# A two-layer GRU with a mixture of experts: products of 256 columns issued as two calls of 128, in both halves of a slot

## The chip, the cores and the metric

The kernel runs on one core of a Trainium2 chip, in float32 throughout. The metric is the device time of one execution in microseconds (us). The engines are named as in the profile: PE is the matrix engine, PEld its weight loads, DVE the vector engine, ACT the scalar engine, POOL the general engine and SP the engine whose queue issues the DMAs.

## The reference, cut to what matters

Batch B = 2, T = 1024 time steps, D = 256 features.

```python
mixed = tanh(x @ W_in.T + b_in + cond)                 # for all steps
h1 = gru_layer(mixed, Wih0, Whh0, bih0, bhh0)          # 1024 steps, one after the other
h2 = gru_layer(h1, Wih1, Whh1, bih1, bhh1)
x = x + (gate * h2 + h2) @ W_out.T + b_out
# the mixture, for each of the 2048 tokens
shared = silu(x @ w1) * (x @ w3) @ w2                  # 512 hidden features
s = sigmoid(concat(x, 0) @ router_W)                   # 8 experts, the top 2 are chosen
routed = sum_e combine[e] * (gelu(x @ W1e[e]) @ W2e[e])
out = x + (shared + routed) / 3
```

In a GRU layer each step needs the state of the step before (`r`, `z` and `n` from `h @ Whh.T`), so 1024 steps of each layer follow each other. Everything else, the mixture above all, can be computed for many steps at once.

## The kernel before, in words

**Slots.** The program is fully unrolled: every instruction is issued once. It is written as a sequence of slots. Slot s holds step s of layer 0 and step s - 19 of layer 1 (`LAG` is 19). On PE a slot is (`pe_slots`): layer 0's step (`recur`), at a few slots a projection for layer 1, then whatever the mixture has planned for "part 0" of the slot, then layer 1's step, at a few slots a projection for layer 0, then the mixture's "part 1". The other engines have the same order. With j = s mod 16, the projections stand at j = 0 and 1 in part 0 (layer 1) and at j = 4 and 12 in part 1 (layer 0). They are 192 columns wide.

**A step.** PE multiplies the state (2 columns of weights per step done in the chunk of 16, up to 32) with the recurrent weights: `recur` issues first the reset gate's product (64 columns, L325) and then the others (128 columns, L333); where `r_first` is false (j = 4 and 12, after slot 896 also 0 and 8) one product of 192 columns does both. DVE transposes the results (L395, L404, L405), ACT takes tanh (L466, L472, L476), DVE scans (L413) and a last DVE scan, L424, makes the new state, for which the next step's product of the same layer waits.

**The mixture.** Steps are cut into groups (`GROUPS`: six of 128 steps, then 112, 80 and 64). When a group's states are there (24 slots after its last step) its mixture begins and is spread over a window of slots as long as the next group: 128 slots for the groups 0 to 4, 112 for group 5, then 80, 64 and 64. A token is a column; a group of 128 steps has TG = 256 of them. One product of the mixture is `by_columns` (L272): four matmuls, one for each strip of 32 output features, with TG columns each. In the trace each matmul is two weight loads and two passes over the columns, so a product is 8 LDWEIGHTS and 8 MATMUL records. A group has 94 products: 4 for the output layer, 2 for the router (one matmul each, not four), 48 `up` and 40 `down`.

**The plan.** `Mixture.add` gives every operation of the mixture a half-slot (two to a slot) by its dependences and by `busy`, which names the half-slots an engine may not use. A group is `sparse` when its window has 128 slots or more, that is the groups 0 to 4: then PE may take part 0 only (and not at j = 0 and 1), ACT part 0 only. A PE operation stands at least two half-slots after an operation of another engine on which it waits. For these groups the plan puts the 94 products in 94 of the 112 allowed part 0 places; part 1 holds none. In the windows of groups 6 to 8 both parts may be used; group 5 has 12 products in part 1.

**SP and the weights of the experts.** When the router's result `comb_t` is there (half-slot 84 of the window), SP writes it to DRAM, and one slot later reads it back to all partitions (`c_all`, 1 MB in the SBUF for 256 tokens). The experts' results wait for it (`mix.transfer`: 12 half-slots).

Of the kernel before, what the change touches and what calls it, by code (L numbers as in the profile page):

```python
# [12 lines left out]
KT = D // P  # L13
# [4 lines left out]
CH = 16  # L18
ROWS = CH * B
# [6 lines left out]
HS, E, HE = 512, 8, 256  # L26
# [22 lines left out]
def projection_pieces(l):  # L49

    return {4: 0, 12: 1} if l == 0 else {0: 0, 1: 1}
# [9 lines left out]
class Mixture:  # L61


    def __init__(self, first, steps, window):
        self.first, self.end, self.steps, self.window = first, first + steps, steps, window
        self.begin = self.end + LAG + 5
        self.sparse = window >= GROUPS[0]
        self.pieces = range(2 if steps > 5 * CH else 1)
        self.y_done = f"y{KT - 1}{self.pieces[-1]}"
        self.ops = {k: [] for k in ("pe", "act", "dve")}  # L70
        self.when, self.value, self.engine, self.signals = {}, {}, {}, {}
# [19 lines left out]
    def busy(self, engine, h):  # L91

        j, part = (h // 2 + self.begin) % CH, h % 2
        if engine == "pe":
            return j in projection_pieces(part ^ 1) or part == 1 and (self.sparse or self.window > 5 * CH and j % 8 != 6)
        if engine == "act":
            return ((j - LAG) if part else j) % CH == 2 or self.sparse and part == 1
        return (j, part) in ((13, 0), (1, 1), (2, 1))
# [22 lines left out]
def gru_moe_kernel(nc, a, out):  # L121
    with ExitStack() as ctx:
# [509 lines left out]
        def mixture_at(eng, engine, s, part, base):  # L632

            mix = in_window(s)
            if mix is None:
                return
            h = (s - mix.begin) * 2 + part
            for at, name, waits, issue in mix.ops[engine]:
                if at != h:
                    continue  # L640
                for w in waits:
                    wait_for(eng, mix, w)
                half = h // mix.window
                if name == "out00" and mix is mixtures[0]:
                    eng.wait_ge(s_mld, 16 * len(late_loads))
                    eng.wait_ge(s_mix, B * NTB * KT)
                if name == "out00" and mix is not mixtures[0]:
                    eng.wait_ge(m_sets[1]["dve"], before(mix).value[before(mix).y_done])
                if name == "out00":
# [21 lines left out]
        def plan(mix, x2, y, mid, score_th, scores, comb_t, c_all, by_tok, top, rest, equal, lead, mask, sel, denom, big, recip,  # L671
# [6 lines left out]
            def tokens(q):  # L678
                return slice(TH * q, TH * q + TH)

            for m in range(KT):
                for kt in range(KT):
                    mix.add("pe", f"out{m}{kt}", (), lambda pe, col, m=m, kt=kt: by_columns(
                        pe, ups[0][:, m], feature_tile(w_out[:, kt], m), hist[:, kt, bass.ds(col + ROWS, TG)], m == kt == 0, kt == KT - 1))
            for m in range(KT):
                for q in mix.pieces:
                    mix.add("dve", f"x2{m}{q}", (f"out{KT - 1}{KT - 1}",), lambda v, col, m=m, q=q: v.scalar_tensor_tensor(  # L687
                        x2[:, m, tokens(q)], ups[0][:, m, tokens(q)], b_out[:, m:m + 1],
                        x_t[:, m, bass.ds(col + TH * q, TH)], ALU.add, ALU.add), even=True)
            for kt in range(KT):  # L690
                mix.add("pe", f"route{kt}", (f"x2{KT - 1}{LAST}",), product(ups[1][0:E, 0], w_r[:, kt], x2[:, kt], kt == 0, kt == KT - 1))
            for b in range(B):
                mix.add("act", f"score{b}", (f"route{KT - 1}",), lambda act, col, b=b: act.activation(
                    score_th[:, b::B], ups[1][0:E, 0, b::B], ACT.Tanh, bias=r_bias[:, b:b + 1], scale=0.5))

            def up(u):
                kind, i = UNITS[u]
                free = () if u == 0 else ("score1",) if u == 1 else (f"act{u - 2}_1" if UNITS[u - 2][0] == "e" else f"hid{u - 2}_{LAST}",)
                for h in range(2):
                    for kt in range(KT):  # L700
                        if kind == "s":
                            w = feature_tile((w_1, w_3)[h][:, kt], i)
                        else:
                            w = feature_tile(w_1e[:, i, kt], h)
                        mix.add("pe", f"up{u}_{h}{kt}", free if h == kt == 0 else (),
                                product(ups[u % 2][:, h], w, x2[:, kt], h == kt == 0, kt == KT - 1))

            def nonlinear(u):
                kind, i = UNITS[u]
                bank, done = ups[u % 2], f"up{u}_{1}{KT - 1}"  # L710
                read = () if u < 2 or kind == "e" and mix is mixtures[-1] else (last_hid(u - 2),)
                if kind == "s":

# [21 lines left out]
            def last_hid(u):  # L735
                return f"hid{u}_{LAST}" if UNITS[u][0] == "s" else f"hid{u}_{KT - 1}{LAST}"
# [11 lines left out]
            def down(u):  # L748
                kind, i = UNITS[u]
                tiles = [w_2[:, i]] if kind == "s" else [w_2e[:, i, kt] for kt in range(KT)]  # L750
                for k, w in enumerate(tiles):
                    for m in range(KT):
                        last = k == len(tiles) - 1 and m == KT - 1
                        name = f"down{u}" if last else f"down{u}_{k}{m}"
                        mix.add("pe", name, (last_hid(u),) if k == m == 0 else (),
                                product(acc[:, m], feature_tile(w, m), hid[u % 2][:, k], u == k == m == 0, u == len(UNITS) - 1 and last))


            per_expert = [32, NB, E]
# [253 lines left out]
```

## Time and profile before

| | us |
|---|---|
| Median of three runs | 2193.89 |
| Lowest and highest | 2191.00, 2194.55 |
| Span of the profiled execution | 2185.8 |
| PE, PEld, DVE, ACT, POOL busy in it | 2068.4, 1485.0, 1841.5, 1201.4, 560.5 |

The page gives no time of the profiled execution apart from its span, from the first to the last instruction. The runs' times hold some 5 to 9 us around the span (2191.00 - 2185.8 to 2194.55 - 2185.8).

A busy PE is not a PE at its peak: matmuls are pipelined and their ends are modelled. What counts for this kernel is how long a slot takes, and what stands in the gaps of PE between one layer's step and the other's. The granted TensorE clock stands at 2.4 GHz, 0.99 to 1.00 of it, in all stretches shown below.

### The profile page before, as it was taken

What the parts mean: (1) busy time and instruction counts of PE and PEld (TensorE: products, weight loads), DVE (VectorE), ACT (ScalarE), POOL (GpSimd) and SP (SyncE); (2) the same over time, 40 slices, a digit from 0 to 9 for tenths busy, and PEclk for the clock granted to TensorE, in tenths of its full rate; (3) what the DMA queues carried; (4) which work ended last, traced back from release to release, by engine and by line L of the source; (5) the groups of instructions that cost most, each with busy time, mean ns of one, the idle gap of its engine ahead of it and who ended that gap; (6) DMA issues with size and microseconds to landing.
All of it is one profiled execution on the core that took longest, in us unless ns stands there. A gap on an engine that the chain in (4) does not pass through costs nothing.

```text
span 2185.8 us, 162058 instructions
## 1 busy us (share of the span) xinstructions
PE 2068.4 (95%) x69920; PEld 1485.0 (68%) x69920; DVE 1841.5 (84%) x11225; ACT 1201.4 (55%) x6471; POOL 560.5 (26%) x2542
## 2 busy tenths in 40 slices
PE   6989899999999999999999999999999999999987
PEld 3666666677666776767767676666767676777766
DVE  4888889888888888888888888888888888888874
ACT  2555555555555555555555555555555555555542
POOL 1222232222322223222222222222232222222220
PEclk9999999999999999999999999999999999999999
DMA  5000000000000000000000000000000000000000
GB/s 219 4 4 5 4 5 5 24 5 5 9 5 24 5 5 10 5 24 5 10 5 24 5 5 9 5 24 5 5 10 5 24 5 10 5 21 9 5 16 19
DMA packets 10879, 32.76 MB, mean 15 GB/s; under 512 B 1368, under 2 KB 6832, under 8 KB 9136
## 3 DMA queue, kind: packets, MB, share of 16 engines
q1 hardware_dynamic: 10160, 22.38, 2.8%
q8 instruction: 548, 8.98, 1.7%
q14 instruction: 171, 1.40, 0.2%
HBM read 20.22 MB, written 2.16 MB: 10 GB/s over the span
## 4 chain that ended last, share of the span: by engine, by line
PE 60%; DVE 26%; ACT 10%; issue 3%; DMA 1%; SPq 0%; POOL 0%; DVEq 0%; POOLq 0%
PE bank L333 29%; PE bank L325 17%; PE bank L272 11%; DVE n_first L404 9%; DVE cells L424 7%; ACT factors L472 6%; ACT cells L476 4%; DVE r_pre L395 4%; DVE z_pre L405 3%; PE bank L306 3%; DVE bank L413 1%; DVE n_second L380 0%; DVE x L687 0%; PE bank L657 0%; DVE hid L745 0%
## 5 line engine op out<-in xcount | busy, mean ns | idle before, releaser
L333 PE MATMUL bank<-w_h,cells 128*22 128x128 f32 (+4 forms) x32768 | 1363.4, 281 | 23.6 <-DVE cells L424 13.9
L333 PEld LDWEIGHTS bank<-w_h,cells 128*22 128x22 f32 (+4 forms) x32768 | 853.0, 111 | 130.5 <-DVE cells L424 91.3
L325 PEld LDWEIGHTS bank<-w_h,cells 128*2 128x2 f32 (+15 forms) x28112 | 512.2, 113 | 528.1 <-DVE cells L424 502.8
L517 POOL TENSOR_SCALAR cells<-cells 128x4 f32<-128x4 f32 x2048 | 463.6, 226 | 1525.8 <-DVE cells L424 1524.8
L325 PE MATMUL bank<-w_h,cells 128*2 128x64 f32 (+15 forms) x28112 | 770.1, 225 | 76.3 <-DVE cells L424 55.5
L466 ACT ACTIVATE n_second<-r_pre 128x4 f32<-128x4 f32 x2048 | 426.3, 208 | 508.8 <-DVE r_pre L395 466.3
L472 ACT ACTIVATE factors<-z_pre 128x4 f32<-128x4 f32 x2048 | 429.6, 210 | 436.5 <-DVE z_pre L405 358.8
L404 DVE STREAM_TRANSPOSE n_first<-bank 128x64 f32<-128x64 f32 x2048 | 600.0, 293 | 33.1 <-PE bank L333 23.7
L424 DVE TENSOR_TENSOR_SCAN cells<-factors,cells 128x18 f32<-128x18 f32 x2048 | 397.2, 194 | 241.5 <-ACT cells L476 177.1
L395 DVE STREAM_TRANSPOSE r_pre<-bank 128x64 f32<-128x64 f32 x2048 | 480.6, 235 | 33.3 <-PE bank L325 24.9
L405 DVE STREAM_TRANSPOSE z_pre<-bank 128x64 f32<-128x64 f32 x2048 | 427.4, 209 | 0.0
L413 DVE TENSOR_TENSOR_SCAN bank<-n_first,n_second 128x12 f32<-128x12 f32 x2048 | 396.7, 194 | 5.3 <-ACT n_second L466 1.1
L476 ACT ACTIVATE cells<-bank 128x8 f32<-128x8 f32 x2048 | 367.6, 180 | 1.4 <-DVE bank L413 0.2
L272 PE MATMUL bank<-x,w_1e 128*32 128x256 f32 (+3 forms) x2304 | 162.3, 357 | 2.3 <-issue 2.3
L272 PE MATMUL bank<-hid,w_2e 128*32 128x256 f32 (+3 forms) x2304 | 157.6, 356 | 1.8 <-DVE hid L745 1.8
L306 PE MATMUL bank<-w_x,stage 128*32 128x192 f32 x2048 | 131.9, 327 | 1.6 <-DVE z_pre L405 0.9
L272 PE MATMUL bank<-x,w 128*32 128x256 f32 (+3 forms) x1152 | 81.9, 356 | 0.2 <-DVE hid L721 0.2
L272 PEld LDWEIGHTS bank<-x,w_1e 128*32 128x32 f32 x2304 | 73.2, 110 | 2.6 <-issue 0.3
L272 PEld LDWEIGHTS bank<-hid,w_2e 128*32 128x32 f32 x2304 | 70.2, 110 | 5.4 <-DVE hid L745 2.4
L306 PEld LDWEIGHTS bank<-w_x,stage 128*32 128x32 f32 x2048 | 63.9, 109 | 14.2 <-DVE z_pre L405 1.4
L745 DVE TENSOR_TENSOR hid<-act_t,c_all 128x128 f32<-128x128 f32 (+2 forms) x240 | 66.4, 277 | 1.2 <-issue 0.7
L478 ACT ACTIVATE bank<-biases 128x256 f32<-128x256 f32 x124 | 47.5, 383 | 0.0
(91 smaller groups left out, 558.8 us busy)
## 6 DMA issues: line engine op xcount, KB each, us to landing
c_all<-weights SPq DMA_DIRECT2D x6, 1024.0 KB
x_t<-in_x_t SPq DMA_DIRECT2D x4, 512.0 KB, 7.4
w_1e<-in_w_1e SPq DMA_DIRECT2D x1, 2048.0 KB
w_2e<-in_w_2e SPq DMA_DIRECT2D x1, 2048.0 KB
w_x<-in_w_x SPq DMA_DIRECT2D x2, 768.0 KB, 8.2
w_h<-in_w_h SPq DMA_DIRECT2D x2, 768.0 KB, 9.5
w<-in_w SPq DMA_DIRECT2D x3, 512.0 KB
out_y<-y SPq DMA_DIRECT2D x6, 256.0 KB, 3.5
```

Of the source, the lines that this page charges most:

```text
L272: mm = pe.matmul(ps[strip], w[:, strip], x, start=start, stop=stop, tile_position=(0, 32 * g), skip_group_check=True)
L325: mm = pe.matmul(r_sums[l][p][32 * g:32 * g + B * (j + 1)], state_tile(l, j, kt), w_h[l][:, kt, g, 2 * U:], start=False, stop=False, tile_ ...
L333: mm = pe.matmul(sums[l][p][32 * g:32 * g + B * (j + 1), 0:width], state_tile(l, j, kt), w_h[l][:, kt, g, 0:width], start=False, stop=Fals ...
L395: v.transpose(r_pre[l][:].rearrange("p i b -> p b i"), blocks(at)).then_inc(s["turn"], 1)
L404: v.transpose(n_first[l][:, :, :, 2].rearrange("p i b -> p b i"), blocks(sums[l][p][:, 0:U])).then_inc(s["for_n"], 1)
L405: v.transpose(z_pre[l][:].rearrange("p i b -> p b i"), blocks(sums[l][p][:, U:2 * U])).then_inc(s["turn"], 1)
L413: v.tensor_tensor_scan(n_scan[l], n_first[l][:, own].rearrange("p i b e -> p (i b e)"), n_second[l][p][:, own].rearrange("p i b e -> p (i ...
L424: v.tensor_tensor_scan(step_cells(l, (j + 1) % CH, 0), factors[l][:, 2:], step_cells(l, j), 0.0, ALU.mult, ALU.add)\
L466: act.activation(n_second[l][p][:, own, :, 0], r_pre[l][:, own], ACT.Tanh, scale=0.5).then_inc(s["for_n"], 1)
L472: act.activation(cell_part(factors[l][:], 2), z_pre[l][:, own_rows(j)], ACT.Tanh, scale=0.5)
L476: act.activation(to, n.to_broadcast([P, B, UB, 2]), ACT.Tanh).then_inc(s["for_h"], 1)
L517: pool.tensor_scalar(cell_part(step_rows(l, j), 3), cell_part(step_rows(l, j), 1), 0.5, None, ALU.mult)\
```

## The change

For the sparse groups only (0 to 4), every product of 256 columns becomes two calls with 128 columns each (`mix.cuts` has two elements, `cut(c)` is the half of the columns). A group then has 188 PE operations, and each call loads its weights anew. `busy` no longer keeps PE out of part 1 for sparse groups: only the projections' places are closed (j = 0 and 1 in part 0, j = 4 and 12 in part 1). The two halves of a product have consecutive places, so that one mostly stands behind layer 0's step and the other behind layer 1's. For the other groups nothing changes (one cut, and the same rule for part 1 as before). ACT and DVE keep their operations and their rules; they wait for the second half of a product.

By the planner's rules the 188 calls get 94 places in part 0 and 94 in part 1; 81 slots of a window have both, 26 have one. Thirteen calls a window stand in part 1 of the slots j = 0 and 1, behind layer 1's projection and step. `comb_t` moves from half-slot 84 to 86, so both of SP's DMAs for it come one slot later, and the last result from half-slot 236 to 240 (of 256), and its store with it.

```diff
         self.sparse = window >= GROUPS[0]
         self.pieces = range(2 if steps > 5 * CH else 1)
+        self.cuts = self.pieces if self.sparse else range(1)
...
         if engine == "pe":
-            return j in projection_pieces(part ^ 1) or part == 1 and (self.sparse or self.window > 5 * CH and j % 8 != 6)
+            return j in projection_pieces(part ^ 1) or part == 1 and 5 * CH < self.window < GROUPS[0] and j % 8 != 6
...
+            TC, CUT = TG // len(mix.cuts), mix.cuts[-1]
+
+            def cut(c):
+                return slice(TC * c, TC * c + TC)
+
             for m in range(KT):
-                for kt in range(KT):
-                    mix.add("pe", f"out{m}{kt}", (), lambda pe, col, m=m, kt=kt: by_columns(
-                        pe, ups[0][:, m], feature_tile(w_out[:, kt], m), hist[:, kt, bass.ds(col + ROWS, TG)], m == kt == 0, kt == KT - 1))
+                for c in mix.cuts:
+                    for kt in range(KT):
+                        mix.add("pe", f"out{m}{c}{kt}", (), lambda pe, col, m=m, kt=kt, c=c: by_columns(
+                            pe, ups[0][:, m, cut(c)], feature_tile(w_out[:, kt], m), hist[:, kt, bass.ds(col + ROWS + TC * c, TC)],
+                            m == kt == c == 0, kt == KT - 1))
...
                 for h in range(2):
-                    for kt in range(KT):
...
-                        mix.add("pe", f"up{u}_{h}{kt}", free if h == kt == 0 else (),
-                                product(ups[u % 2][:, h], w, x2[:, kt], h == kt == 0, kt == KT - 1))
+                    for c in mix.cuts:
+                        for kt in range(KT):
...
+                            mix.add("pe", f"up{u}_{h}{c}{kt}", free if h == kt == c == 0 else (),
+                                    product(ups[u % 2][:, h, cut(c)], w, x2[:, kt, cut(c)], h == kt == c == 0, kt == KT - 1))
...
-                bank, done = ups[u % 2], f"up{u}_{1}{KT - 1}"
+                bank, done = ups[u % 2], f"up{u}_{1}{CUT}{KT - 1}"
...
                     for m in range(KT):
-                        last = k == len(tiles) - 1 and m == KT - 1
-                        name = f"down{u}" if last else f"down{u}_{k}{m}"
-                        mix.add("pe", name, (last_hid(u),) if k == m == 0 else (),
-                                product(acc[:, m], feature_tile(w, m), hid[u % 2][:, k], u == k == m == 0, u == len(UNITS) - 1 and last))
+                        for c in mix.cuts:
+                            last = k == len(tiles) - 1 and m == KT - 1 and c == CUT
+                            name = f"down{u}" if last else f"down{u}_{k}{m}{c}"
+                            mix.add("pe", name, (last_hid(u),) if k == m == c == 0 else (),
+                                    product(acc[:, m, cut(c)], feature_tile(w, m), hid[u % 2][:, k, cut(c)], u == k == m == c == 0,
+                                            u == len(UNITS) - 1 and last))
```

The router's products are cut in the same way.

## Rows read from the trace of the kernel before

**Rows 1.** The page: its span, PE's records, and the chain's shares by engine.

```profile
span 2185.8 us, 162058 instructions
...
PE 2068.4 (95%) x69920; PEld 1485.0 (68%) x69920; DVE 1841.5 (84%) x11225; ACT 1201.4 (55%) x6471; POOL 560.5 (26%) x2542
...
PE 60%; DVE 26%; ACT 10%; issue 3%; DMA 1%; SPq 0%; POOL 0%; DVEq 0%; POOLq 0%
```

**Rows 2.** Timeline: start, length, engine, line, operation; idle time before in brackets.

```profile
1004.21 0.61 PE L272 MATMUL bank<-x,w_1e 128*32 128x256 f32 x8
...
1004.61 0.25 PEld L325 LDWEIGHTS bank<-w_h,cells 128*6 128x6 f32 x16 [0.27 <-DVE cells L424]
...
1004.86 0.62 PE L333 MATMUL bank<-w_h,cells 128*6 128x128 f32 x16
```

**Rows 3.** Stretches: length, each engine's busy time (records); layer 1's last 16 steps, alone.

```profile
2119.52:2151.63 32.11, 21.54 (x672) 15.65 (x672) 16.97 (x89) 9.72 (x51) 4.10 (x19) 1.00 0.01 3
```

**Rows 4.** The same view: slots 32 to 151, then the five windows of 128 slots.

```profile
81.84:321.79 239.95, 215.43 (x7449) 146.78 (x7448) 203.18 (x1231) 134.92 (x736) 65.71 (x298) 1.00 0.02 5
321.79:581.67 259.88, 253.83 (x8677) 180.44 (x8676) 227.34 (x1397) 149.54 (x807) 69.86 (x316) 1.00 0.03 10
581.67:842.12 260.45, 254.62 (x8677) 180.98 (x8676) 227.48 (x1397) 148.29 (x806) 69.66 (x316) 1.00 0.03 10
842.12:1107.56 265.44, 257.13 (x8677) 184.12 (x8676) 227.84 (x1396) 148.50 (x806) 69.61 (x316) 0.99 0.03 10
1107.56:1371.42 263.86, 255.04 (x8676) 181.60 (x8676) 227.95 (x1396) 148.52 (x806) 69.62 (x316) 1.00 0.03 10
1371.42:1635.85 264.43, 256.57 (x8677) 183.13 (x8676) 228.26 (x1396) 148.75 (x806) 69.72 (x316) 0.99 0.03 10
```

**Rows 5.** The same view, of the scans L424 alone: their number in slots 32 to 151.

```profile
81.84:321.79 239.95, 46.96 (x240) 1.00 0.02 5
```

**Rows 6.** Stretches of two slots (j = 9, 10): no product, 256 columns, 160 twice, 224 twice.

```profile
1935.59:1939.54 3.95, 3.48 (x128) 2.43 (x128) 3.34 (x22) 2.20 (x12) 0.90 (x4) 1.00 0.05 14
648.75:652.68 3.93, 3.93 (x148) 2.85 (x144) 3.69 (x24) 2.12 (x12) 0.91 (x4) 1.00 0.03 6
2068.79:2072.74 3.95, 3.90 (x160) 3.29 (x160) 3.58 (x25) 2.21 (x12) 0.91 (x4) 1.00 0.02 6
1969.16:1973.21 4.05, 4.05 (x160) 3.47 (x160) 3.84 (x26) 2.40 (x14) 0.91 (x4) 1.00 0.02 4
```

**Rows 7.** Single slots j = 0: without and with 256 columns in the slot before.

```profile
597.80:599.74 1.94, 1.88 (x72) 1.43 (x72) 1.62 (x12) 1.10 (x6) 0.95 (x5) 1.00 0.00 0
629.91:631.89 1.98, 1.98 (x76) 1.44 (x72) 1.92 (x13) 1.14 (x7) 0.95 (x5) 1.00 0.03 8
```

**Rows 8.** Single slots j = 2: without products, and with 160 columns behind slot 1's projection.

```profile
2087.01:2089.00 1.99, 1.71 (x68) 1.24 (x64) 1.73 (x12) 1.06 (x6) 0.46 (x2) 1.00 0.87 277
2053.84:2055.93 2.09, 2.09 (x88) 1.83 (x84) 2.03 (x13) 1.31 (x7) 0.46 (x2) 1.00 0.00 0
```

**Rows 9.** A group's busy us and mean ns; instruction queue (packets, MB): page, first window.

```profile
L272 PEld LDWEIGHTS bank<-x,w_1e 128*32 128x32 f32 x2304 | 73.2, 110 | 2.6 <-issue 0.3
...
q8 instruction: 548, 8.98, 1.7%
...
q8 instruction: 68, 1.11, 1.8%
```

**Rows 10.** Waits of PEld in the third, fourth and fifth window: us, times, longest.

```profile
PEld bank L325 <- issue: 3.1, 3, 2.7
...
PEld bank L325 <- issue: 2.4, 1, 2.4
...
PEld bank L325 <- issue: 3.1, 3, 2.5
```

**Rows 11.** DMA share in tenths, 929.5 to 943 in 40 slices; timeline of what follows.

```profile
DMA  0000210000000009599999851100000000020000
...
940.35 0.31 PEld L325 LDWEIGHTS bank<-w_h,cells 128*8 128x8 f32 x14 [2.73 <-issue]
```

More of the change, by code:

```diff
@@ L643, in mixture_at @@
                 half = h // mix.window
-                if name == "out00" and mix is mixtures[0]:
+                if name == "out000" and mix is mixtures[0]:
                     eng.wait_ge(s_mld, 16 * len(late_loads))
                     eng.wait_ge(s_mix, B * NTB * KT)
-                if name == "out00" and mix is not mixtures[0]:
+                if name == "out000" and mix is not mixtures[0]:
                     eng.wait_ge(m_sets[1]["dve"], before(mix).value[before(mix).y_done])
-                if name == "out00":
+                if name == "out000":
                     eng.wait_ge(sets[1][mix.end // CH % 2]["pool"] if mix is not mixtures[-1] else s_hist, 2)
@@ L679, in tokens @@
                 return slice(TH * q, TH * q + TH)
+            TC, CUT = TG // len(mix.cuts), mix.cuts[-1]
+            def cut(c):
+                return slice(TC * c, TC * c + TC)
             for m in range(KT):
-                for kt in range(KT):
-                    mix.add("pe", f"out{m}{kt}", (), lambda pe, col, m=m, kt=kt: by_columns(
-                        pe, ups[0][:, m], feature_tile(w_out[:, kt], m), hist[:, kt, bass.ds(col + ROWS, TG)], m == kt == 0, kt == KT - 1))
+                for c in mix.cuts:
[3 more added lines that the diff above has]
+                            m == kt == c == 0, kt == KT - 1))
             for m in range(KT):
                 for q in mix.pieces:
-                    mix.add("dve", f"x2{m}{q}", (f"out{KT - 1}{KT - 1}",), lambda v, col, m=m, q=q: v.scalar_tensor_tensor(
+                    mix.add("dve", f"x2{m}{q}", (f"out{KT - 1}{CUT}{KT - 1}",), lambda v, col, m=m, q=q: v.scalar_tensor_tensor(
                         x2[:, m, tokens(q)], ups[0][:, m, tokens(q)], b_out[:, m:m + 1],
                         x_t[:, m, bass.ds(col + TH * q, TH)], ALU.add, ALU.add), even=True)
-            for kt in range(KT):
-                mix.add("pe", f"route{kt}", (f"x2{KT - 1}{LAST}",), product(ups[1][0:E, 0], w_r[:, kt], x2[:, kt], kt == 0, kt == KT - 1))
+            for c in mix.cuts:
+                for kt in range(KT):
+                    mix.add("pe", f"route{c}{kt}", (f"x2{KT - 1}{LAST}",),
+                            product(ups[1][0:E, 0, cut(c)], w_r[:, kt], x2[:, kt, cut(c)], kt == c == 0, kt == KT - 1))
             for b in range(B):
-                mix.add("act", f"score{b}", (f"route{KT - 1}",), lambda act, col, b=b: act.activation(
+                mix.add("act", f"score{b}", (f"route{CUT}{KT - 1}",), lambda act, col, b=b: act.activation(
                     score_th[:, b::B], ups[1][0:E, 0, b::B], ACT.Tanh, bias=r_bias[:, b:b + 1], scale=0.5))
@@ L699, in up @@
                 for h in range(2):
[L700 to L704, printed above, removed]
-                        mix.add("pe", f"up{u}_{h}{kt}", free if h == kt == 0 else (),
-                                product(ups[u % 2][:, h], w, x2[:, kt], h == kt == 0, kt == KT - 1))
+                    for c in mix.cuts:
+                        for kt in range(KT):
+                            if kind == "s":
+                                w = feature_tile((w_1, w_3)[h][:, kt], i)
+                            else:
+                                w = feature_tile(w_1e[:, i, kt], h)
+                            mix.add("pe", f"up{u}_{h}{c}{kt}", free if h == kt == c == 0 else (),
+                                    product(ups[u % 2][:, h, cut(c)], w, x2[:, kt, cut(c)], h == kt == c == 0, kt == KT - 1))
             def nonlinear(u):
                 kind, i = UNITS[u]
-                bank, done = ups[u % 2], f"up{u}_{1}{KT - 1}"
+                bank, done = ups[u % 2], f"up{u}_{1}{CUT}{KT - 1}"
                 read = () if u < 2 or kind == "e" and mix is mixtures[-1] else (last_hid(u - 2),)
@@ L752, in down @@
                     for m in range(KT):
-                        last = k == len(tiles) - 1 and m == KT - 1
-                        name = f"down{u}" if last else f"down{u}_{k}{m}"
-                        mix.add("pe", name, (last_hid(u),) if k == m == 0 else (),
-                                product(acc[:, m], feature_tile(w, m), hid[u % 2][:, k], u == k == m == 0, u == len(UNITS) - 1 and last))
+                        for c in mix.cuts:
+                            last = k == len(tiles) - 1 and m == KT - 1 and c == CUT
[3 more added lines that the diff above has]
+                                            u == len(UNITS) - 1 and last))
             per_expert = [32, NB, E]
```

## The prediction

> **What bounds the kernel now.** I read the page's chain first: PE holds 60% of it, DVE 26%, ACT 10% [rows 1]. That looks like a kernel bound by PE, where smaller or better placed products would pay. So the next view is one slot of the timeline. A product of 256 columns stands behind layer 0's step (0.61 us), and yet PE's weight loads then sit idle for 0.27 us until layer 1's scan L424 has made the state [rows 2]. PE waits for the recurrence, not the other way round. The third view is layer 1 alone, after layer 0 has ended: 16 steps in 32.11 us, 2.007 us a step [rows 3]. Now both layers together, with no product of the mixture on PE: slots 32 to 151 hold 240 scans, so 120 slots [rows 5], in 239.95 us [rows 4], 2.000 us a slot. One layer alone is no faster than two: a slot's length is the latency of one step through PE, DVE and ACT, and the other layer and the mixture live in its gaps.
>
> The change touches the five windows of 128 slots. At 2.000 us a slot each would last 255.95 us. They last 259.88, 260.45, 265.44, 263.86 and 264.43 us [rows 4]. The excess is 3.9, 4.5, 9.5, 7.9 and 8.5, together 34.3 us. That is all that could be won in them, whatever is done to the mixture, and 1.6% of the span of 2185.8 us [rows 1].
>
> **What the excess is made of.** Not the columns: two slots without a product take 3.95 us, two with 256 columns in part 0 take 3.93 us [rows 6]. It is in the waits named "issue", in which PE waits for nothing that a semaphore shows. At L325 alone they make 3.1 us in three waits in the third window; the longest one of the third, fourth and fifth window is 2.7, 2.4 and 2.5 us [rows 10]. The one of 2.7 us explains the mechanism: the broadcast of `c_all` fills the DMA engines for the ten slices that start with a 9 and end with a 1 (0.34 us each, 934.6 to 937.9), and PE stands until 940.35 [rows 11]. What PE lacks is instructions. The instruction queue q8 moved 548 packets with 8.98 MB [rows 9], that is 16 KB each; PE and PEld together have 2 x 69,920 = 139,840 records [rows 1], over 548 that is 255. I read a packet as a block of 256 PE instructions. An instruction stream of 124.1 records a slot without products ((7449 + 7448) / 120) costs no excess, one of 135.6 with them ((8677 + 8676) / 128) costs 34.3 us in 640 slots [rows 4]. I take the long waits (2.7 + 2.4 + 2.5 = 7.6 us) as collisions with `c_all`'s DMA, and the other 26.7 us as blocks that came a little late.
>
> The Trainium skill has a rule that speaks the other way: the page "Runtime: NRT & Kernel Launch", section "Instruction fetch mechanics", says that the sequencer loads 16 KiB blocks of 256 instructions ahead of time and that crossing a block is "mostly hidden". The block's size agrees with this trace (16 KB, 255 records); that it is hidden does not, by the issue waits just named. By that rule the term for late blocks below would be 0 and the time that of the second rival.
>
> **The change part by part.**
>
> *Columns and weight loads on PE.* The four strips' 128-column passes of L333, 16 records, take 0.62 us; the 256-column product, 8 records, 0.61 us [rows 2]. Sixteen records of 128 columns move as many columns as eight of 256, so a product cut in two costs PE 0.01 us more, and its eight further weight loads (110 ns each [rows 9], overlapping the passes) run beside. 470 products x 0.01 = 5 us of PE time, beside waits of 0.27 us a slot half: 0 on the path. Without that cover it would be 5 us.
>
> *Part 0 gets shorter.* A 256-column product pushes layer 1's step, and where a short slot follows this shows: j = 0 takes 1.98 us with a product in the slot before, 1.94 without [rows 7]. The plan has 6 such places a window, 30 in all: 30 x 0.045 = -1.4 us. Elsewhere the push costs nothing (3.93 against 3.95 us). After this layer 0's latency is what stands, unchanged.
>
> *Part 1 gets 128 columns.* The trace has no 128-column product behind layer 1's step, but it has wider ones: two slots with 160 columns in both parts take 3.95 us, as long as none; with 224 columns in both 4.05 us [rows 6]. So the gap closes between 160 and 224 and 128 fits: 0 for 405 of the 470 new places. The bound above is a tenth of the 224-column price per slot, 0.05 / 5 = 0.01 us, 4 us in all. The other 65 (13 a window) stand behind layer 1's projection and step at j = 0 and 1. Behind such a one with 160 columns the slot took 2.09 instead of 1.99 us [rows 8]. For 128 columns between 0 and 0.10; I take the half, 65 x 0.05 = +3.3 us (0 to 6.5).
>
> *The instruction stream.* 92 of the 94 products add 16 records, the router's two add 4: 1480 a window, 11.6 a slot, from 135.6 to 147.1; 7400 in all, 29 blocks more on some 340. This is the term that decides. Lower bound: the same lateness per block, 26.7 x 29 / 340 = +2.3 us. Upper bound: the excess went from 0 at 124.1 to 26.7 us at 135.6 records, so another 11.6 on a straight line add +27 us; and nothing says that it is straight, since 81 slots a window now hold 160 records where the fullest held 144. Against it, the slots with 160 records that the trace has (the last three groups) mostly ran at full speed, as the 3.95 us for two shows [rows 6]. I take +12, nearer to the stretch that resembles it less and further from the line, because those slots had shorter runs and fewer records at j = 0 and 8.
>
> *The broadcast.* It comes one slot later and meets blocks in another phase. It lasts 3.4 us [rows 11]; a block will last 256 / 147.1 x 2.0 = 3.5 us. So nearly every window has one block whose load starts inside, waiting on average half of it, 1.7 us, 8.5 us in five, against 7.6 now. I take 0, from -7 (all windows miss) to +6.
>
> *Moved steps on other engines.* The engines' counts don't change; SP's two DMAs for `comb_t` and the store move by one and two slots, and nothing waits behind them for as long; the experts' product still has its 12 half-slots. ACT waits for a last half at the same distance. 0.
>
> **Sum.** -1.4 + 0 + 3.3 + 12 + 0 = +14 us on the span of 2185.8, 2199.7; the runs lay 8.1 us above the span at their median, so 2193.89 + 14 = 2208 us.
>
> **Rivals.**
> 1. *Starved blocks.* In a run of slots with 160 records each block comes late and the delay sustains itself. If it costs 0.1 us in each of the 405 slots with both calls, it adds 40 us: 2235 us. For it speaks how steeply the excess rose from 124 to 136 records [rows 4]; against it the 160-record pairs [rows 6].
> 2. *Hidden blocks.* Lateness per block stays as it is: -1.4 + 3.3 + 2.3, 2198 us, or with smaller part 1 prices 2194 us: no change. For it speak the same pairs. With blocks hidden it is the page's rule cited above.
> 3. *The phase, on the other side: faster.* A window now loads 68 blocks (68 packets [rows 9]), a whole number, so blocks fall at nearly the same places in every window, and three windows of five lose 2.4 to 2.7 us at `c_all` [rows 10]. With 1480 / 256 = 5.8 more the phase moves by a fifth of a block a window. If the broadcast then meets no block in most windows (-6), the late blocks stay as they are or fall with the phase (-5), and part 1 costs nothing (-1.4): 2182 us. It decides if the gain in phase exceeds what 29 blocks more cost.
> 4. *Part 1 is too tight.* 128 columns delay layer 0's step by 0.05 us in most slots: 470 x 0.05 = +23, with the rest 2225 us. Against it: 160 columns cost nothing [rows 6].
> 5. *The edit does not do what it says*: PE keeps the same columns per call. The plan leaves no room for that; 1 in 100, and counted with rival 2.
>
> **How the numbers follow.** The forecast (2199 to 2222) gets 0.48, rival 1 0.14, rival 2 0.18, rival 3 0.13, rival 4 0.07. Within 0.2% is 2189.5 to 2198.3 us, about what a measurement of this kernel can tell from no change. Slower by more: the forecast, rivals 1 and 4, and a few hundredths of rival 2: 0.72. Same: 0.15. Faster: 0.13. The range takes in rival 2, the near half of rival 3 and rival 1 without its tail: 2187 to 2237 us.
>
> **What the profile after would show.** L272 with 1472 records a window on PE and as many on PEld, all of 128 columns; PE and PEld records of 147 a slot; q8 with 577 packets. If the sum is right: pairs j = 9, 10 without an issue wait at 3.95 us, slots j = 1 and 2 some 0.05 us longer, j = 0 at 1.94 us; more issue waits of 0.1 to 0.5 us in the windows, their excess 8 to 12 us each; windows of other groups unchanged. Wrong would be: pairs without issue waits above 3.97 us (rival 4), issue waits in most blocks (rival 1), or fewer and shorter ones than now (rival 3).

## The result, and the profile after

The changed kernel takes 2265.93 us (median of four runs, 2261.83 to 2274.76) against 2193.92 us for the kernel before in the same comparison: a ratio of 1.0334 [1.0311, 1.0356], 72 us slower. The direction was forecast, the size was not: 2208 us was forecast, and 2265.93 lies above the upper end of the range, 2237 us.

The page of the changed kernel: span, each engine's busy time with its records, the instruction queue, and the chain's shares.

```profile
span 2260.0 us, 169453 instructions
...
PE 2103.8 (93%) x73620; PEld 1607.1 (71%) x73620; DVE 1854.5 (82%) x11225; ACT 1208.8 (53%) x6471; POOL 560.4 (25%) x2542
...
q8 instruction: 576, 9.44, 1.7%
...
PE 67%; DVE 20%; ACT 8%; issue 4%; DMA 1%; SPq 0%; POOL 0%; DVEq 0%; POOLq 0%
```

DVE, ACT and POOL have the records they had [rows 1]; PE and PEld have 3700 more each, which is the 7400 forecast. The span grew by 74.2 us. Stretches of the changed kernel, with the same columns as [rows 4]: slots 32 to 151, the five windows of 128 slots, and the window of group 5.

```profile
82.30:322.53 240.23, 215.69 (x7449) 146.91 (x7448) 203.37 (x1231) 135.09 (x736) 65.73 (x298) 1.00 0.02 5
322.53:597.05 274.52, 260.99 (x9417) 205.26 (x9416) 229.96 (x1397) 150.75 (x807) 69.77 (x316) 1.00 0.03 10
597.05:868.87 271.82, 260.59 (x9416) 204.80 (x9416) 229.68 (x1396) 150.36 (x806) 69.68 (x316) 1.00 0.03 10
868.87:1146.69 277.82, 262.11 (x9417) 205.84 (x9416) 230.65 (x1396) 150.02 (x806) 69.68 (x316) 1.00 0.03 10
1146.69:1426.47 279.78, 261.21 (x9417) 205.15 (x9416) 230.00 (x1397) 150.24 (x806) 69.64 (x316) 1.00 0.03 10
1426.47:1703.38 276.91, 261.83 (x9416) 205.53 (x9416) 230.20 (x1396) 150.12 (x806) 69.62 (x316) 1.00 0.03 10
1703.38:1937.36 233.98, 227.31 (x7652) 165.60 (x7652) 200.31 (x1233) 130.18 (x708) 61.37 (x277) 1.00 0.03 10
```

Slots 32 to 151, where there is no mixture, take what they took. The five windows take 1703.38 - 322.53 = 1380.85 us instead of 1635.85 - 321.79 = 1314.06, so 66.8 of the 74.2 us are in them. Group 5's window, whose instructions are the same, took 230.47 us before, in the row below, and takes 233.98 now; that leaves 4 us for everything else. Over 128 slots at this trace's bare length (128 / 120 x 240.23 = 256.25 us) the windows are 18.3, 15.6, 21.6, 23.5 and 20.7 us longer, together 99.6, where it was 34.3. In the rest of this text that sum is called the excess, and each trace's own slots 32 to 151 give its bare length.

Group 5's window in the trace of the kernel before:

```profile
1635.85:1866.32 230.47, 224.75 (x7652) 163.24 (x7652) 199.57 (x1233) 130.63 (x708) 61.39 (x277) 1.00 0.03 11
```

PE stands in the waits named "issue". PEld's waits in the third window of the changed kernel (us in all, times, longest):

```profile
PEld bank L334 <- issue: 8.2, 15, 0.9
PEld bank L326 <- issue: 7.2, 16, 1.0
...
PEld bank L273 <- issue: 3.1, 7, 0.6
PEld bank L307 <- issue: 0.9, 2, 0.7
```

They add up to 19.4 us in 40 waits, nearly the whole excess of this window (21.6), and none is longer than 1.0 us. The window holds (9417 + 9416) / 256 = 73.6 blocks, so over half of all blocks came late. The next view is the timeline of PEld in a stretch with both calls in most slots, and the instruction queue in the same stretch (packets, MB, share).

```profile
1302.98 0.33 PEld L334 LDWEIGHTS bank<-w_h,cells 128*2 128x2 f32 x16 [1.11 <-issue]
...
1307.09 0.24 PEld L334 LDWEIGHTS bank<-w_h,cells 128*30 128x30 f32 x8 [0.91 <-issue]
...
1309.77 0.38 PEld L334 LDWEIGHTS bank<-w_h,cells 128*8 128x8 f32 x15
1311.00 0.09 PEld L334 LDWEIGHTS bank<-w_h,cells 128*8 128x8 f32 x1 [0.85 <-issue]
...
q8 instruction: 3, 0.05, 2.2%
```

Three stops, 4.11 and 3.91 us apart. The second splits the 16 loads of one step into 8 and 8, the third cuts off the last of 16: no semaphore stands there, only the border of a block of 256 instructions, and three packets of 16 KB came for three stops. At 160 records a slot of 2 us, a block without a stop would last 3.2 us. The stretches around them show what a slot costs with a stop and without one; first two slots (j = 13 and 14) without, then single slots with one each:

```profile
1295.59:1299.57 3.98, 3.98 (x164) 3.36 (x160) 3.68 (x24) 2.20 (x12) 0.91 (x4) 1.00 0.01 4
...
1301.59:1304.64 3.05, 2.13 (x88) 1.72 (x80) 1.71 (x12) 1.10 (x6) 0.95 (x5) 1.00 0.04 8
1306.57:1309.46 2.89, 2.37 (x93) 2.13 (x96) 1.73 (x12) 1.29 (x7) 0.45 (x2) 1.00 0.03 6
1309.46:1312.29 2.83, 2.26 (x92) 1.79 (x84) 1.84 (x13) 1.35 (x8) 0.75 (x4) 1.00 0.02 6
```

The two calls in a slot cost nothing as work: 3.98 us for two slots. A border inside costs the slot 0.8 to 1.05 us.

I counted single records of both whole traces: of the gaps over 0.15 us on PE or PEld that no semaphore ended, 69 of 79 before and 323 of 339 after stand at one and the same place (a load and the matmul beside it) in every 256 instructions of PE. That place is the border. In the five windows the gaps there without a semaphore sum to 26.4 us before and 97.7 after, beside an excess of 34.3 and 99.6. Before, 85 of 340 blocks came more than 0.06 us late, now 217 of 369, by 0.45 us in the mean. In the changed kernel the first instruction of a late block mostly runs 2.3 to 2.9 us (median 2.5) after the start of the 16 KB transfer that brought it, though the transfer itself takes 1.1 us. In the changed kernel that transfer starts, at the median of the late blocks, 153 instructions ahead of the border. At 147.1 instructions in 2.0 us these last 2.08 us, 0.4 less than the 2.5 needed. Before, it was 172 instructions at 135.6 in 2.0 us, 2.54 us against 2.6: on the edge.

Counted from the other side, a late block's load started 1.1 us (median, in both traces) after the first instruction of the block ahead of it. With the 2.5 us behind it, a block's own work must last some 3.6 us (an estimate from these two medians) if the next is to come in time. In the changed kernel 155 of the 188 borders behind a block with less than 3.3 us of work were late, but 16 of the 104 behind one with 3.7 us or more; before, 10 of 23 and 15 of 154. So the cut did not so much add 29 blocks as make 188 of them short, where 23 were. That is how 29 more blocks could cost 65 us.

### The profile page after: what moved, and what is told of

Its sections match the earlier page's. It is cut to its first block, busy times and chain, and to the rows that moved or that the text cites. A ratio compares the mean times of both kernels' runs of the same rounds, so it can differ in the third digit from the quotient of the medians.

```text
span 2260.0 us, 169453 instructions
## 1 busy us (share of the span) xinstructions
PE 2103.8 (93%) x73620; PEld 1607.1 (71%) x73620; DVE 1854.5 (82%) x11225; ACT 1208.8 (53%) x6471; POOL 560.4 (25%) x2542
## 4 chain that ended last, share of the span: by engine, by line
PE 67%; DVE 20%; ACT 8%; issue 4%; DMA 1%; SPq 0%; POOL 0%; DVEq 0%; POOLq 0%
PE bank L334 32%; PE bank L326 19%; PE bank L273 13%; DVE n_first L405 7%; DVE cells L425 5%; ACT factors L473 4%; DVE r_pre L396 3%; ACT cells L477 3%; PE bank L307 3%; DVE z_pre L406 2%; DVE bank L414 1%; DVE n_second L381 0%; DVE x L695 0%; DVE bank L377 0%; DMA c_all<-weights 0%
## 5 line engine op out<-in xcount | busy, mean ns | idle before, releaser
L334 PE MATMUL bank<-w_h,cells 128*22 128x128 f32 (+4 forms) x32768 | 1405.6, 281 | 42.0 <-issue 24.9
L334 PEld LDWEIGHTS bank<-w_h,cells 128*22 128x22 f32 (+4 forms) x32768 | 878.6, 111 | 148.7 <-DVE cells L425 73.1
L326 PE MATMUL bank<-w_h,cells 128*2 128x64 f32 (+15 forms) x28112 | 801.5, 225 | 92.4 <-DVE cells L425 56.3
L326 PEld LDWEIGHTS bank<-w_h,cells 128*2 128x2 f32 (+15 forms) x28112 | 538.6, 114 | 444.4 <-DVE cells L425 380.7
L273 PE MATMUL bank<-x,w_1e 128*32 128x128 f32 (+3 forms) x3584 | 209.3, 288 | 1.6 <-issue 1.2
L273 PE MATMUL bank<-hid,w_2e 128*32 128x128 f32 (+3 forms) x3584 | 204.9, 291 | 5.2 <-issue 2.5
L273 PEld LDWEIGHTS bank<-x,w_1e 128*32 128x32 f32 x3584 | 124.8, 110 | 6.7 <-issue 3.9
L273 PEld LDWEIGHTS bank<-hid,w_2e 128*32 128x32 f32 x3584 | 121.3, 111 | 11.3 <-issue 6.1
L273 PE MATMUL bank<-x,w 128*32 128x128 f32 (+3 forms) x1792 | 103.9, 288 | 1.2 <-issue 0.7
L273 PEld LDWEIGHTS bank<-x,w 128*32 128x32 f32 x1792 | 60.6, 110 | 5.2 <-issue 3.5
```

Source lines behind the costliest of these rows:

```text
L326: mm = pe.matmul(r_sums[l][p][32 * g:32 * g + B * (j + 1)], state_tile(l, j, kt), w_h[l][:, kt, g, 2 * U:], start=False, stop=False, tile_ ...
L334: mm = pe.matmul(sums[l][p][32 * g:32 * g + B * (j + 1), 0:width], state_tile(l, j, kt), w_h[l][:, kt, g, 0:width], start=False, stop=Fals ...
```

## The experiments

Each group of runs had its own runs of the kernel before (2180.89, 2195.01 and 2182.94 us at the median), and ratios are against those alone. "Records a slot" are PE's and PEld's in the five windows.

**Group 1: places, instructions or columns? (before: 2180.89 us)**

*Both calls in part 0*, so that nothing is moved but every call is cut:

```diff
+            def in_calls(ps, w, x, start, stop):
+                def issue(pe, col):
+                    for c in range(CALLS):
+                        mm = product(ps[:, cut(c)], w, x[:, cut(c)], start and c == 0, stop)(pe, col)
...
-                mix.add("pe", f"route{kt}", (f"x2{KT - 1}{LAST}",), product(ups[1][0:E, 0], w_r[:, kt], x2[:, kt], kt == 0, kt == KT - 1))
+                mix.add("pe", f"route{kt}", (f"x2{KT - 1}{LAST}",), in_calls(ups[1][0:E, 0], w_r[:, kt], x2[:, kt], kt == 0, kt == KT - 1))
```

with `by_columns`, `up` and `down` in the same way.

> The kernel before, with each product of the five sparse groups issued as two calls of 128 columns back to back in its old place in part 0; part 1 stays empty. It has the changed kernel's PE records (147 a slot) but not its places. Theory (PE lacks instructions: a block of 256 comes too late when a slot holds many records): 2245 to 2275 us, like the changed kernel. Rival (128 columns behind layer 1's step delay layer 0): 2189 to 2200 us, like before.

Measured: 2241.32 us, 4 us below the range expected from late blocks; ratio 1.0288 [1.0261, 1.0316], excess 82.5 us. Without one call moved, most of the loss is there. It lay a little below the changed kernel's 1.0334, which had been measured elsewhere; whether the places cost the rest is settled in group 3.

*Only `up` cut in two* (the same `in_calls`, for the 48 `up` products alone), half of the added records:

> As e1_part0, but only the 48 'up' products of a sparse group are issued as two calls: 768 records more a window instead of 1480, 141.6 a slot. Theory of late blocks: between before and changed, 2215 to 2240 us. Rival (places): 2189 to 2200 us.

Measured: 2202.76 us, 12 us below the range expected from late blocks; ratio 1.0114 [1.0085, 1.0142], excess 42.6 us with 141.6 records a slot. One of its windows, to be held against [rows 4]:

```profile
588.48:853.58 265.10, 257.09 (x9061) 193.91 (x9060) 227.98 (x1396) 148.45 (x806) 70.21 (x316) 1.00 0.03 10
```

The first 6.0 records a slot cost 2202.76 - 2180.89 = 22 us, the next 5.5 (with the kernel of the run before) 2241.32 - 2202.76 = 39 us: 3.6 us a record, then 7.0, no straight line.

*The changed kernel's places with two strips of four*, so that the record count is that of before. Half of each 128-feature product of groups 0 to 4 is left out:

```diff
+            STRIPS = range(2 if mix.sparse else NQ)
...
-                            m == kt == c == 0, kt == KT - 1))
+                            m == kt == c == 0, kt == KT - 1, STRIPS))
```

against the changed kernel, with `by_columns` running `for g in strips`, and `STRIPS` passed in `up` and `down` too.

> The changed kernel with the same 188 places and 128 columns a call, but in the sparse groups each call computes only the first two of its four strips of output features (the other half of each product is left out, so the output is not the reference's). Its PE records are about those of before, 135.6 a slot, while the columns of a strip still stream in both parts. Theory of late blocks: 2185 to 2205 us. Rival (places): near the changed kernel, 2250 to 2270 us. If strips run one behind the other, PE also has half the work, which would help under both.

Measured: 2175.84 us, 9 us below the range expected from late blocks; ratio 0.9983 [0.9972, 0.9994], excess 18.7 us. Two of its windows:

```profile
584.55:845.25 260.70, 254.34 (x8681) 197.29 (x8680) 228.90 (x1397) 150.37 (x806) 70.14 (x316) 1.00 0.03 10
845.25:1104.99 259.74, 253.38 (x8682) 196.82 (x8680) 228.39 (x1397) 149.97 (x806) 70.09 (x316) 1.00 0.03 10
```

All 188 calls stand in both parts, 13 of them behind layer 1's projection, and the kernel is as fast as before or faster. So the places as such cost nothing. This kernel moves half the strips as well, so alone it doesn't say whether PE's work or its records matter, nor that four strips fit in part 1; the borders counted in the trace of the changed kernel say the first, as the gaps stand there, and group 3 the second.

*One matmul of 128 features for each product*, the kernel before with fewer instructions:

```diff
+        def full_width(pe, ps, w, x, start, stop):
+            return pe.matmul(ps, w, x, start=start, stop=stop, skip_group_check=True)
...
-            return lambda pe, col: by_columns(pe, ps, w, x, start, stop)
+            return lambda pe, col: full_width(pe, ps, w, x, start, stop)
```

with the output layer's products in the same way, in all groups.

> The kernel before, with each product of the mixture (all groups) issued as one matmul of 128 features instead of four of 32: 4 records instead of 16, 127 a slot in the windows. Theory of late blocks: the excess of 34 us in the five windows falls to 0 to 12, and the later windows gain some 10: 2150 to 2175 us. Rival: if late blocks are not what costs, 2185 to 2200 us. Against both, one full-width pass could hold PE longer than four strips that overlap; then the slots with a product are longer than 1.97 us without any issue wait.

Measured: 2295.56 us, ratio 1.0535 [1.0513, 1.0557]: a clear miss. The gaps at the borders did fall, to 8.0 us in the five windows, but something else rose. Its third window, PEld's waits in it, and a product on the timeline:

```profile
868.99:1142.88 273.89, 268.37 (x8124) 186.60 (x8124) 228.32 (x1396) 146.45 (x806) 70.11 (x316) 1.00 0.03 9
...
PEld bank L268 <- issue: 19.4, 92, 0.3
...
1050.30 0.30 PEld L268 LDWEIGHTS bank<-hid,w_2e 128*128 128x128 f32 x2 [0.29 <-issue]
1050.30 0.70 PE L268 MATMUL bank<-hid,w_2e 128*128 128x256 f32 x2
```

There is a wait ahead of each of the 92 products that are wider than 32 features, 0.21 us in the mean. It is not at borders and has nothing to do with late blocks. Group 2 follows it.

**Group 2: the width of a strip, and the broadcast (before: 2195.01 us)**

The changed kernel itself again, as the reference of this group:

> The changed kernel itself once more, on one chip with the following kernels and beside before. With both calls in part 0 the ratio to before was 1.029 (e1_part0). If places in part 1 cost nothing, as with half the strips (e3_two_strips), the ratio is 1.029 here too, 2240 us where before takes 2180. If the places of the calls cost something of their own at this number of records, it is 1.033 as at first, 2253 us.

Measured: 2275.48 us, ratio 1.0356 [1.0321, 1.0391]. Against the 1.0288 of both calls in part 0, in group 1, that looks like a price of the places; group 3 puts the two side by side.

*Two matmuls of 64 features for each product*, the kernel before, and the same in the changed kernel:

```diff
+        def by_pairs(pe, ps, w, x, start, stop):
+            for g in range(NQ // 2):
+                strip = slice(64 * g, 64 * g + 64)
+                mm = pe.matmul(ps[strip], w[:, strip], x, start=start, stop=stop, tile_position=(0, 64 * g),
+                               skip_group_check=True)
+            return mm
```

> The kernel before, with each product of the mixture issued as two matmuls of 64 features instead of four of 32: 8 records instead of 16, 130 a slot in the windows. Theory of late blocks: their share of the excess falls by half or more, -10 to -20 us. The one full-width matmul (e4_full_width) had hardly late blocks but held PE longer, +5%. If the price lies in the length of a 64-wide pass, this one costs between: 2190 to 2250 us. If it lies in the change between 32-wide strips and another width, it costs nearly as much as full width, 2270 us. If neither, 2160 to 2172 us where before takes 2180.

> The changed kernel (two calls of 128 columns, both parts) with two matmuls of 64 features a call: 16 records a product, as before, 135.6 a slot. Theory of late blocks: no more of them than before. Where a change of width costs, it is paid twice as often as in e6_pairs: above it. If nothing but records counts: 2172 to 2185 us where before takes 2180.

Measured: 2272.75 us, ratio 1.0344 [1.0312, 1.0377], and 2357.54 us, ratio 1.0732 [1.0691, 1.0772]. PEld's waits in the third window, of the kernel before with pairs:

```profile
PEld bank L270 <- issue: 19.6, 93, 0.3
```

and of the changed kernel with pairs:

```profile
PEld bank L271 <- issue: 37.4, 183, 0.3
PEld bank L333 <- issue: 23.1, 135, 0.2
```

It is not the full width alone that costs; 64 features do too, among strips of 32: 0.20 to 0.21 us ahead of nearly each product, and in the changed kernel, which has two calls for each, twice as many waits, with further ones as the stream goes back to strips of 32. The gaps at the borders are nearly gone in both (5.2 and 3.7 us). So the pair of runs can't say what the change would cost with fewer instructions: the cure costs more than the illness.

*The broadcast in four DMAs*, one a slot, the kernel before (`mix.spreads` is 4 for the sparse groups and 1 for the others):

```diff
-                if m == mix.when["comb_t"] // 2 + 1:
-                    sp.wait_ge(spread, 16)
-                    sp.dma_start(c_all[:, :, 0:n], weights[:, 0:n].partition_broadcast(P)).then_inc(spread, 16)
+                k = m - mix.when["comb_t"] // 2 - 1
+                if 0 <= k < mix.spreads:
+                    sp.wait_ge(spread, 16 * (k + 1))
+                    some = slice(E // mix.spreads * k, E // mix.spreads * (k + 1))
+                    sp.dma_start(c_all[:, some, 0:n], weights[some, 0:n].partition_broadcast(P)).then_inc(spread, 16)
...
-            mix.transfer("spread", "comb_t", 12)
+            mix.transfer("spread", "comb_t", 16 if mix.sparse else 12)
```

> The kernel before, with the 1 MB broadcast of c_all in the five sparse groups cut into four DMAs of two experts each, one after the other, and four half-slots more before the experts' results use it. Each fills the DMA engines for 0.85 us instead of 3.4. Theory (an instruction block that falls into the broadcast waits for its end): the waits of 2.4 to 2.7 us at it shrink below 1 us, 4 to 8 us faster than before. Rival (those waits have another cause): no change.

Measured: 2190.93 us, ratio 0.9979 [0.9962, 0.9997]. The third window of this kernel, and PEld's waits in it:

```profile
847.23:1107.05 259.82, 254.02 (x8677) 180.87 (x8676) 227.68 (x1397) 148.93 (x806) 70.11 (x316) 1.00 0.03 10
...
PEld bank L334 <- issue: 1.3, 3, 0.5
PEld bank L273 <- issue: 0.3, 1, 0.3
PEld bank L326 <- issue: 0.3, 1, 0.3
```

Where the kernel before had a wait of 2.7 us [rows 10] the longest is 0.5, and in none of the five windows is an issue wait of PEld longer than 0.8. That the long waits were collisions with the broadcast is shown. The gain is 4 us, hardly clear of noise, and not the 7.6 us of those three waits: the excess of the five windows came to 33.0 us in this trace, with 7.7 and 9.1 in two later windows, though no long wait was left. A stop that is taken away moves every later border, and part of the gain may be lost again there; no run shows that.

**Group 3: the places once more, and breaks in the dense runs (before: 2182.94 us)**

Both calls in part 0, and the changed kernel, side by side:

> e1_part0 (two calls back to back in part 0) beside the changed kernel on one chip, to settle whether the places add anything at 147 records a slot. If records alone count, both have one ratio to before, 1.03 to 1.035. If both parts in use make blocks later than calls in pairs do, this one is 5 to 15 us faster than the changed kernel.

> The changed kernel beside e1b_part0_again. Ratio to before 1.033 to 1.036, as in both earlier measurements.

Measured: 2249.74 us, ratio 1.0315 [1.0293, 1.0337], and 2251.87 us, ratio 1.0317 [1.03, 1.0334]. The same window in the one and in the other:

```profile
874.84:1148.64 273.80, 261.72 (x9418) 206.45 (x9416) 229.05 (x1397) 148.42 (x806) 70.17 (x316) 1.00 0.03 10
```

```profile
875.79:1149.14 273.35, 261.47 (x9417) 205.47 (x9416) 229.82 (x1397) 150.52 (x806) 70.14 (x316) 1.00 0.03 10
```

The places make no difference that these runs can tell; the cut alone is the loss, and four strips fit in part 1 (rival 4 falls).

*Part 0 closed to the mixture at j = 8 or 2 in turn*, the kernel before: its runs of slots with a product become shorter, the sum of the instructions stays.

```diff
         if engine == "pe":
+            if self.sparse and j == (8, 2)[(h // 2 + self.begin) // CH % 2]:
+                return True
```

> The kernel before, with PE's part 0 closed to the mixture in the sparse groups at j = 8 of one chunk of 16 slots and j = 2 of the next: the 94 products stay, at the same 16 records each, but a run of seven full slots is broken by one with 128 records. Theory (a late block makes the next one late, and a slot with fewer records lets the loads catch up): 2 to 8 us faster than before. Rival (only the mean number of records counts): no change. A cost on the other side: the last result stands in the window's last half-slot.

Measured: 2179.89 us, ratio 0.9984 [0.9974, 0.9995], excess 16.3 us, gaps at borders 18.3. The trace of before, which is of the first comparison, has 34.3 and 26.4, but by the times the gain is 3 us: one execution's excess is only roughly that of another's. Part of the step is in the bare length: this trace's slots 32 to 151 took 241.17 us, and against the 239.95 of before its excess would be 22.8.

*The same with the broadcast in four DMAs:*

> e9_breaks and e8_four_spreads together. If both act on different waits, their gains add: 4 us from the broadcast and 2 to 8 from the breaks, 6 to 12 us faster than before.

Measured: 2173.45 us, ratio 0.9958 [0.9944, 0.9972], 9.5 us or 0.4% faster than the kernel before and the fastest of all. Two of its windows:

```profile
844.04:1104.09 260.05, 254.56 (x8680) 181.62 (x8676) 227.43 (x1396) 148.46 (x806) 69.90 (x316) 1.00 0.04 10
1104.09:1362.95 258.86, 254.12 (x8680) 181.33 (x8676) 226.67 (x1397) 147.93 (x806) 69.96 (x316) 1.00 0.04 10
```

The same records as in the third and fourth window of before [rows 4], in 260.05 and 258.86 us where that trace has 265.44 and 263.86.

**All together.** The gaps at borders in the five windows, by records a slot. The rows are single executions of three groups, and differ by a quarter at the same kernel; the steps between the counts are larger than that. The bare lengths run from 239.95 to 241.17 us, which alone moves an excess by up to 6.5 us.

| records a slot | kernel | gaps at borders, us | excess, us |
|---|---|---|---|
| 127 | one matmul of 128 features | 8.0 | (waits for the width) |
| 130 | pairs of 64 features | 5.2 | (waits for the width) |
| 135.6 | before | 26.4 | 34.3 |
| 135.6 | two strips, places of after | 19.0 | 18.7 |
| 135.6 | breaks; breaks and four DMAs | 18.3; 14.5 | 16.3; 17.8 |
| 135.6 | four DMAs | 26 | 33.0 |
| 141.6 | only `up` cut | 36.3 | 42.6 |
| 147.1 | all cut, in part 0 (two traces) | 75.3, 92.5 | 82.5, 100.7 |
| 147.1 | changed kernel (three traces) | 97.7, 118.3, 93.2 | 99.6, 118.4, 92.8 |

## Why the prediction was right and wrong

**What bounds the kernel: right.** The slot's length is the latency of the recurrence, 2.00 us, and undisturbed slots did not change. Two slots j = 9 and 10 of the changed kernel with both calls in each, to be held against [rows 6]:

```profile
599.01:602.96 3.95, 3.95 (x168) 3.29 (x160) 3.37 (x22) 2.17 (x12) 0.91 (x4) 1.00 0.02 4
```

**Part 0 shorter, -1.4 us: right, and too small to matter.** Slots j = 0 without a late block now have a median of 1.94 us, as the one that had no product in the slot before it [rows 7]. (Those rows give 0.04 us a place and -1.2 in all, the sum took 0.045.)

**Part 1 at no cost: right.** The changed places with few records, and half the strips, are no slower than before (0.9983), and both calls in part 0 cost the same as the changed places (1.0315 and 1.0317).

**The 65 places behind layer 1's projection, +3.3 us: too high.** Two single slots of the changed kernel, j = 1 with both calls and a projection, and j = 2 behind it:

```profile
751.90:753.89 1.99, 1.99 (x88) 1.70 (x84) 1.66 (x12) 1.04 (x6) 0.45 (x2) 1.00 0.04 12
753.89:755.89 2.00, 1.85 (x75) 1.43 (x71) 1.73 (x11) 1.29 (x7) 0.45 (x2) 1.00 0.00 0
```

The 2.09 us of 160 columns [rows 8] does not carry over to 128; the medians of the slots j = 1 and j = 2 that have no late block in them or in the slot before moved by less than 0.02 us each. The lower end of the range was the right value.

**The instruction stream, +12 us: the step that failed.** The excess of the five windows rose by 99.6 - 34.3 = 65.3 us. The mechanism was the one named, blocks of 256 that come late, and the count was right (576 packets against 577). The size was taken from the 160-record pairs that ran at 3.95 us [rows 6], and with them the value was placed below the straight line's 27 us. Those pairs, with 320 records each, do hold a border (at 2070.49 us in the one of 3.95 us), but one whose block came in time; the changed kernel has such a pair too (3.98 us), ahead of slots of 3.05 and 2.89. Such a pair tells what the work costs, and not how often a block is late. The question was how long a block's instructions last against how long its load needs, and before's trace had the answer in its late blocks: 2.6 us from the start of a load to the first instruction, against the 2.54 us that 172 instructions last. With a quarter of all blocks already late, the term had to be worked as "how many more cross the edge, and by how much", not as a share of the old loss. The warning that nothing says the line is straight was in the text, but neither the sum nor the upper bound acted on it.

**Rival 1, starved blocks: the right case with too small a price.** It said 0.1 us in each of 405 slots; measured are 65.3 / 405 = 0.16. Of its two parts, that most blocks have a wait is seen (217 of 369). That one late block makes the next one late is not shown: 146 late blocks follow a late one, where 217 x 217 / 369 = 128 would do so by chance. Breaks in the dense runs helped before's stream by 0.16%, which fits either reading.

**The broadcast, 0 from -7 to +6: within its bounds.** The long waits, 2.7, 2.4 and 2.5 us in the third to fifth window before [rows 10], are 1.5 us in the first and 2.1 in the fourth now, and at most 1.0 in the others. That is 4 us less, but in the two later traces of the changed kernel the gaps of over 1.4 us right behind the broadcasts sum to 9.2 and 6.1 us: which windows are hit differs between executions. The term was real (0.21% when the DMA is cut in four) and small beside the other.

**Rivals 2, 3 and 4 fall.** The Trainium skill's "mostly hidden" ("Runtime: NRT & Kernel Launch", section "Instruction fetch mechanics") holds at 127 to 130 records a slot, with 5 to 8 us of gaps in 640 slots, and not at 147, with 75 to 118 us. No phase made the kernel faster in any of three traces. Rival 4's sign was pairs j = 9 and 10 above 3.97 us without an issue wait; only two pairs with both calls are free of late blocks in the trace, and they took 3.95 and 3.94 us. The two kernels of group 3 speak more strongly against it. (Its 2225 us is no sum of its own terms: with 2.3 us for the stream they give 2222, with 12 us 2231.)

**Group 5's window**, forecast unchanged, is 3.5 us longer with the same instructions (230.47 to 233.98 us). The gaps at its borders account for it: they sum to 2.7 us before and 6.2 after.

**Left open.** Why more of group 5's blocks are late was not followed; its borders fall elsewhere than before, but that this is the reason is only argued. Weight loads double together with the instructions, and no run here separates them; that the gaps stand at the borders and the undisturbed slots did not grow speaks for the instructions. And what decides when a block's load starts was not found: mostly 0.3 to 1.6 us after the first instruction of the block ahead.

## What to carry to other kernels

In this unrolled program PE's instructions are a resource with a rate. Count them per stretch and compare how long a block of 256 lasts with what the next one needs (here 1.1 us until its load begins and 2.5 more until its first instruction): near the edge 8% more instructions nearly tripled the loss, from 34.3 to 99.6 us or 3.3% of the time, and pieces that would be free as work are not. Cutting the products to fill gaps doubled their instructions and bought nothing here; what brought a little was to spread the instructions that there are, and to cut up the large DMA that the blocks have to pass (together 0.9958 [0.9944, 0.9972]). And a stretch that ran undisturbed prices the work in it, never the queue behind it.

## What was not expected of the hardware

A product whose strips have another width than its neighbours (64 or 128 features among strips of 32) is preceded by a wait of about 0.2 us named "issue": 92 waits and 19.4 us, 93 and 19.6, 183 and 37.4 in a window of 128 slots, and the kernels were 3.4 to 7.3% slower. The Trainium skill says in "TensorEngine Tiling (Array Packing)", section "Key Properties", that a change of the tiling mode drains the engine; these waits agree with it, and give it a price in this kernel.

A late block's transfer takes 1.1 us, but its first instruction runs 2.3 to 2.9 us after the transfer began, so most of the way is not the moving of the bytes.
